# Four convolution layers on eight images: the stores of an image moved into its last convolution, and the matmuls of a strip pair put in another order

## What is computed

```
x = x + irfftn(complex 3x3 convolution of rfftn(norm(x)))   # layer 0
x = x + gate(norm(x))                                       # layer 1: rows and halves of the channels are let through or not
x = x + conv3x3(norm(x), W)                                 # layer 2
x = x + conv3x3(norm(x), weight)                            # layer 3
```

## Time and profile before, and how to read them

| | kernel before |
|---|---|
| median of three runs | 4691.74 us |
| the profiled execution's own time | 4709.38 us |
| its span, from the first to the last instruction | 4707.6 us |
| TensorE busy | 4279.1 us (91% of the span) |
| VectorE busy | 3334.5 us (71%) |
| ScalarE busy | 2540.4 us (54%) |
| mean granted TensorE clock | 0.971 of full speed |
| data read and written in HBM | 323.60 MB and 134.22 MB |

### The profile page before, as it was taken

The page is one execution under the profiler, slowest core; times in us unless marked ns, Lnnn a source line. Parts: engine busy times, 40 slices in busy tenths (PEclk is TensorE's granted clock), DMA queues, the critical chain, the costliest instruction groups (busy, mean ns, idle before and its releaser), DMA issues.

```text
span 4707.6 us, 229463 instructions
## 1 busy us (share of the span) xinstructions
PE 4279.1 (91%) x85024; PEld 2675.9 (57%) x85024; DVE 3334.5 (71%) x13348; ACT 2540.4 (54%) x8637; POOL 1.0 (0%) x6
## 2 busy tenths in 40 slices
PE   4999988999999998999989999899998999988898
PEld 1455765556655566555655566555665557655476
DVE  2887757876578765887658875688756887578863
ACT  4675526655266543666436654366633666345562
POOL 0000000000000000000000000000000000000000
PEclk8999999999999999999999999999999999999999
DMA  7442015620155202651035510356003650034204
GB/s 190 130 136 76 4 40 171 189 89 4 49 185 182 74 3 62 187 186 54 3 85 183 183 38 3 94 181 187 27 3 108 186 181 14 3 109 139 88 4 146
DMA packets 290246, 468.06 MB, mean 99 GB/s; under 512 B 25536, under 2 KB 92288, under 8 KB 289408
## 3 DMA queue, kind: packets, MB, share of 16 engines
q1 hardware_dynamic: 289536, 457.92, 32.4%
HBM read 323.60 MB, written 134.22 MB: 97 GB/s over the span
## 4 chain that ended last, share of the span: by engine, by line
PE 60%; DVE 12%; DMA 8%; issue 8%; SPq 5%; ACT 3%; DVEq 1%; ACTq 1%
PE ps L1361 34%; PE ps L1255 9%; DMA raw<-x 8%; PE ps L1270 5%; PE ps L1263 3%; PE ps L1279 3%; PE ps L1125 2%; DVE shared L858 2%; SPq L426 2%; SPq L433 2%; DVE xin L853 1%; DVE shared L854 1%; SPq L407 1%; ACT x L584 1%; DVE xin L852 1%
## 5 line engine op out<-in xcount | busy, mean ns | idle before, releaser
L1361 PE MATMUL ps<-x,conv_s 32*32 32x512 f32 x49104 | 1741.9, 606 | 62.4 <-DVE x L1087 30.0
L1361 PEld LDWEIGHTS ps<-x,conv_s 32*32 32x32 f32 x49104 | 1242.5, 104 | 509.5 <-issue 273.7
L1255 PE MATMUL ps<-shared 32*32 32x512 f32 x16384 | 657.4, 604 | 0.0
L1270 PEld LDWEIGHTS ps<-hil,shared 128*128 128x128 f32 x4096 | 504.6, 194 | 194.0 <-issue 193.2
L662 ACT ACTIVATE x<-ps,vec 128x256 f32<-128x256 f32 x512 | 214.6, 470 | 741.4 <-PE ps L1361 741.4
L584 ACT ACTIVATE x<-ps,vec 128x128 f32 (+1 forms) x1024 | 377.6, 385 | 432.2 <-PE ps L1270 431.2
L858 DVE SCALAR_TENSOR_TENSOR shared<-xin,trig 128x128 f32<-128x128 f32 x2048 | 533.8, 301 | 106.7 <-DVE shared L854 98.8
L1279 PE MATMUL ps<-eye,vsb 128*128 128x128 f32 x2048 | 370.7, 305 | 237.1 <-DVE vsb L879 134.1
L1270 PE MATMUL ps<-hil,shared 128*128 128x128 f32 x4096 | 572.5, 284 | 0.0
L1086 DVE SCALAR_TENSOR_TENSOR x<-ps,x 128x256 f32<-128x256 f32 x512 | 214.8, 420 | 427.2 <-ACT x L662 426.2
L1255 PEld LDWEIGHTS ps<-shared 32*32 32x32 f32 x16384 | 310.3, 104 | 278.8 <-issue 213.2
(11 more groups left out here) (204 smaller groups left out, 4711.7 us busy)
## 6 DMA issues: line engine op xcount, KB each, us to landing
out<-x SPq DMA_DIRECT2D x512, 256.0 KB
shared<-x SPq DMA_DIRECT2D x448, 256.0 KB
raw<-x SPq DMA_DIRECT2D x256, 256.0 KB
raw<-x SPq DMA_DIRECT2D x512, 128.0 KB
shared<-t_strip SPq DMA_DIRECT2D x512, 96.0 KB, 4.0
x<-x SPq DMA_DIRECT2D x64, 256.0 KB, 8.8
x<-t_proj SPq DMA_DIRECT2D x1, 2048.0 KB, 11.8
trig<-t_trig SPq DMA_DIRECT2D x1, 512.0 KB, 12.1
```

The costliest lines, as they stand in the source:

```text
L1255: mm = pe.matmul(ps[TM * cg:TM * cg + TM, bank, :], wst[TM * rg:TM * rg + TM, k, v, a, :], of[TM * rg:TM * rg + TM, :], start=(a == AXS), ...
L1270: mm = pe.matmul(quarter(ps[:, BY + 2 * odd + e, :], int(q < 2), q % 2), xt[:, e, q, :], hil[:, q, 0:P], start=False, stop=True, skip_grou ...
L1361: mm = pe.matmul(halves(ps[TM * cg:TM * cg + TM, banks[k], :]), conv_s[TM * rg:TM * rg + TM, kw, second, :], x1b[TM * rg:TM * rg + TM, of, ...
```

## The change

It changes four things. SyncE: of an image's 64 strips, 56 are stored in its own third convolution and the last 8 in the next first layer; the loads of the next image's pairs 0, 1 and 2 stand before the first store, after 36 stores and after 48 stores. TensorE: `add_u` takes one strip, and the order is, for each strip, row term, Hilbert product, transposes; the wait for the eviction stands before each strip's first products in `mix`. ScalarE: `turned_out` of the first strip stands before both `evict`. VectorE: in `make_planes`, `minus` is made before `plus`, the full wait at the weights becomes a wait for all but the last step, and the next image's planes are made at pairs 17 and 23 of the third convolution.

```
--- before.py
+++ after.py
@@ -27,7 +27,8 @@
 GROUPS = STRIPS // GROUP
 STORE_SEMS = 4
 STORES = 16 * STRIPS // STORE_SEMS
-DEFERRED = STRIPS - 2 * UNROLL
+DEFERRED = 2 * UNROLL
+STORED_BY = (36, 48, STRIPS - DEFERRED)
 SIDE = HALF + 2
 WIDE = 2 * SIDE
 PAIRS = STRIPS // 2
@@ -39,7 +40,7 @@
 GATES_AHEAD = 3 * GROUP
 GATE_STEPS = 3 * GROUP + 2
 RAW = 2
-U_AT, C_AT, PLANES_AT = (5, 8), (12, 14, 16), (20, 22)
+U_AT, C_AT, PLANES_AT = (5, 8), (12, 14, 16), (17, 23)
 DOT_CREDIT = 2
 
 
@@ -416,14 +417,13 @@
             for k in range(STORE_SEMS):
                 sp.sem_inc(c_stored[k], STORES)
 
-            def store(i, s):
-
-                k = s % STORE_SEMS
+            def store(i, s, k, turn):
+
                 sp.wait_ge(evicted, ev(i, 1 + STRIPS + s + 1))
                 sp.sem_inc(s_sp, 1)
-                sp.wait_ge(c_stored[k], (i + 1) * STORES + s // STORE_SEMS * 16)
+                sp.wait_ge(c_stored[k], (i + 1) * STORES + turn * 16)
                 sp.sem_inc(s_sp, 1)
-                sp.dma_start(out[i].rearrange("c (s r) w -> s r c w", r=ROWS)[s], x1[:, s, 0:N]).then_inc(c_stored[k], 16)
+                sp.dma_start(out[i].rearrange("c (s r) w -> s r c w", r=ROWS)[s], x1[:, bass.ds(s, 1), 0:N]).then_inc(c_stored[k], 16)
 
             def load_next(image, s, t, k):
 
@@ -438,7 +438,7 @@
                     sp.wait_ge(a_projected, j * LANDING + (k - LANDING + 1 + A_CREDIT))
                     land(j * LANDING + k, k)
 
-            for pair in range(2):
+            for pair in range(AHEAD):
                 load_pair(0, pair, 2 * pair)
 
             def image(i, more, stores_left):
@@ -454,27 +454,27 @@
                 if more:
                     sp.wait_ge(p_cols, 3 * i + 1)
                     sp.sem_inc(s_sp, 1)
-                for pair in range(2, AHEAD):
-                    load_pair(i, pair, 2 * pair)
-                for pair in range(DEFERRED // 2):
+                for pair in range(PAIRS):
                     feed(pair, 2 * pair % TABLES)
-                    if stores_left:
+                    if stores_left and pair < DEFERRED // 2:
                         for e in range(2):
-                            store(i - 1, STRIPS - DEFERRED + pair * 2 + e)
-                for pair in range(PAIRS - UNROLL, PAIRS):
-                    feed(pair, 2 * pair % TABLES)
+                            s = STRIPS - DEFERRED + pair * 2 + e
+                            store(i - 1, s, s % STORE_SEMS, s // STORE_SEMS)
+
+                def stores(first, last):
+
+                    with sp.Fori(first // STORE_SEMS, last // STORE_SEMS) as j:
+                        for k in range(STORE_SEMS):
+                            store(i, j * STORE_SEMS + k, k, j)
+
                 if more:
-                    for pair in range(2):
+                    stored = 0
+                    for pair, until in enumerate(STORED_BY):
                         load_pair(i + 1, pair, 2 * pair)
-
-                for n in range(PAIRS):
-                    if more and n >= PAIRS - (STRIPS - DEFERRED):
-                        sp.wait_ge(evicted, ev(i, 1 + STRIPS + 2 * n + 2))
-                        sp.sem_inc(s_sp, 1)
-                        store(i, n - (PAIRS - (STRIPS - DEFERRED)))
-                    elif not more:
-                        for e in range(2):
-                            store(i, 2 * n + e)
+                        stores(stored, until)
+                        stored = until
+                else:
+                    stores(0, STRIPS)
 
             image(0, True, False)
             with sp.Fori(1, B - 1) as i:
@@ -608,9 +608,10 @@
                 def step(t, odd, uses):
 
                     copy_v(t)
+                    turned_out(t * 2, 0)
                     for e in range(2):
                         evict(t * 2 - 2 + e, e, BY + 2 * (1 - odd) + e, 2 * (1 - odd) + e, uses)
-                        turned_out(t * 2 + e, e)
+                    turned_out(t * 2 + 1, 1)
                     squares(t * 2 - 2, 2 * (1 - odd), uses)
 
                 copy_v(0)
@@ -849,17 +850,20 @@
                     dve.wait_ge(x_loaded[e], (i * PAIRS + pair + 1) * (16 + 16 * e))
                     dve.wait_ge(mixed, i * PAIRS + pair - 1 + MIXED_CREDIT)
                     plus, minus = xin[:, k, 0:HALF], xin[:, k, HALF:N]
-                    b.did(V.scalar_tensor_tensor(plus, raw[:, e, 0:HALF], v1(MEAN2), raw[:, e, HALF:N], ALU.subtract, ALU.add))
-                    V.tensor_tensor(minus, raw[:, e, 0:HALF], raw[:, e, HALF:N], ALU.subtract).then_inc(x_taken, 1)
-                    b.then(V.scalar_tensor_tensor(fg(wst[:, k]), fg(mix_s[:, 1]), row_trig[:, 0, bass.ds(s, 1)], fg(mix_s[:, 0]), ALU.mult, ALU.add))
-                    dve.wait_ge(x_taken, i * STRIPS + s + 1 + RAW)
+                    b.did(V.tensor_tensor(minus, raw[:, e, 0:HALF], raw[:, e, HALF:N], ALU.subtract))
+                    V.scalar_tensor_tensor(plus, raw[:, e, 0:HALF], v1(MEAN2), raw[:, e, HALF:N], ALU.subtract, ALU.add).then_inc(x_taken, 1)
+                    b.did(V.scalar_tensor_tensor(fg(wst[:, k]), fg(mix_s[:, 1]), row_trig[:, 0, bass.ds(s, 1)], fg(mix_s[:, 0]), ALU.mult, ALU.add))
+                    b.settle(but=1)
                     for a in range(2):
                         for q in range(2):
                             b.did(V.scalar_tensor_tensor(quarter(planes[:, a, k, :], q, 0), split_in(minus)[:, q, :], 1.0, split_in(trig[:, a, 0:HALF])[:, q, :],
                                                          ALU.mult, ALU.mult, accum_out=gsum[:, 2 * a + q, bass.ds(s, 1)]))
+                        if a == 0:
+                            dve.wait_ge(x_taken, i * STRIPS + s + 1 + RAW)
                         ins = V.tensor_tensor(planes[:, a, k, HALF:N], plus, trig[:, a, 0:HALF], ALU.mult)
                         if a == 0:
                             b.did(ins)
+                            b.settle(but=3)
                             b.did(V.scalar_tensor_tensor(fg(wst[:, k]), fg(mix_s[:, 2]), row_trig[:, 1, bass.ds(s, 1)], fg(wst[:, k]), ALU.mult, ALU.add))
                     ins.then_inc(planes_ready, 1)
                     assert b.n == DVE_B, b.n
@@ -1239,13 +1243,14 @@
 
                     pe.wait_ge(planes_ready, t0 + t * 2 + 2)
                     due()
-                    pe.wait_ge(y_evicted, t0 + t * 2 - 2) if type(t) is not int or t > 1 else None
-                    due()
                     for e in range(2):
                         pe.wait_ge(v_copied[e], i * PAIRS + t) if type(t) is not int or t > 0 else None
                         due()
                     for a in (AXS, AXB, AXC):
                         for e in range(2):
+                            if a == AXS and (type(t) is not int or t > 1):
+                                pe.wait_ge(y_evicted, t0 + t * 2 - 3 + e)
+                                due()
                             k = 2 * odd + e
                             for v in range(2):
                                 for rg in range(TILES):
@@ -1256,12 +1261,11 @@
                                                    start=(a == AXS), stop=(v == 1 and a == AXC), skip_group_check=True)
                     mm.then_inc(mixed, 1)
 
-                def add_u(t, odd, table, uses):
-
-                    for e in range(2):
-                        pe.wait_ge(tab_loaded[table + e], (i * (STRIPS // TABLES) + uses + 1) * 16)
-                        pe.matmul(ps[:, BY + 2 * odd + e, :], strip[HP * e:HP * e + HP, table + e, 0:P], u[HP * e:HP * e + HP, :],
-                                  start=False, stop=False, skip_group_check=True)
+                def add_u(e, odd, table, uses):
+
+                    pe.wait_ge(tab_loaded[table + e], (i * (STRIPS // TABLES) + uses + 1) * 16)
+                    pe.matmul(ps[:, BY + 2 * odd + e, :], strip[HP * e:HP * e + HP, table + e, 0:P], u[HP * e:HP * e + HP, :],
+                              start=False, stop=False, skip_group_check=True)
 
                 def hilbert(s, e, odd):
 
@@ -1289,8 +1293,8 @@
                 def step(t, odd, uses, table, table_uses, first=False):
 
                     mix(t, odd)
-                    add_u(t - 1, 1 - odd, table, table_uses)
                     for e in range(2):
+                        add_u(e, 1 - odd, table, table_uses)
                         hilbert(t * 2 - 2 + e, e, 1 - odd)
                         turn(t, e)
                     project_next(2 * (1 - odd), table, uses, first)
@@ -1310,8 +1314,8 @@
                         step(j * 4 + 1 + k, (k + 1) % 2, j * 2 + k // 2, 2 * k, j)
                 for t in range(PAIRS - 3, PAIRS):
                     step(t, t % 2, (t - 1) // 2, 2 * (t - 1) % TABLES, STRIPS // TABLES - 1)
-                add_u(PAIRS - 1, 1, TABLES - 2, STRIPS // TABLES - 1)
                 for e in range(2):
+                    add_u(e, 1, TABLES - 2, STRIPS // TABLES - 1)
                     hilbert(STRIPS - 2 + e, e, 1)
```

## The result

The kernel after takes 4747.7 us (median of 4 runs, 4741.4 to 4751.9), the kernel before 4693.7 beside it (4 runs, 4676.9 to 4716.7). The ratio is 1.0104, with a 95% interval of 1.0076 to 1.0132: slower by some 50 us, twice the 23 us that a measurement can tell.

A forecast was written before the change was run, and what follows sets the result against it. TensorE, busy for 91% of the span, was taken as the bound. First layer -12.6, third-convolution stores +41 and planes +26 gave +54 us: 4763.8 against the profiled execution, 4746 against the median; range 4620 to 4805.

The forecast's parts named there:

- The row terms apart: First layer, TensorE: each strip's row term runs alone at 1.06 us, making the step 9.6 us.
- the second row term is cheap: Rival, first layer: the second term costs less than its 1.06 us; 4623 at half, 4499 at nothing; chance 0.20.
- ScalarE's order: First layer: copying the first transposes before the evictions ends the waits on L577; later evictions cost nothing in images 0 to 6.
- I leave 0.15 of it: First layer of image 7: of mix's 0.90 and 0.98 us wait for the second eviction, 0.15 stays; step 8.74.
- The first two intervals: Start of the first layer, images 1 to 6: the first two mix-to-mix intervals stay at 23.4 us together.
- The stores in the third convolution: Third convolution, images 0 to 6: TensorE stalls among the stores, 5.9 us an image, 41 in seven.
- likeliest reading: Third convolution: TensorE's six unexplained stalls in image 7, 6.7 us, are code fetches coming late among the stores.
- fetches stay hidden: Rival, third convolution: code fetches cost nothing, so without the 41 us the kernel takes 4705; chance 0.17.
- stores starve the third convolution: Rival, third convolution: stalls three times image 7's and late pair 1 planes, 82 us more, 4828; chance 0.10.
- The planes apart: Third convolution: planes at pairs 17 and 23 cost two waits and clock falls, 3.7 us an image, 26 in seven.
- Planes fit: Rival, third convolution: with the blocks apart both waits vanish, -40 in place of +26 us, 4680; chance 0.08.
- VectorE's wait at nothing: First layer: removing VectorE's full wait, 0.39 us a pair, gains nothing unless the step came below 8.4 us.

The follow-up runs named there:

- experiment 1: The changed kernel with both strips' row terms ahead of the first Hilbert product again, all else as changed: 4565.4 us, 0.972 of the kernel before.
- Experiment 2: The changed kernel with the DMA queue's order of before, 56 strips stored in the next first layer: 4788.4 us, 1.0188 of the kernel before.
- experiment 8: The changed kernel with the row terms together again and two stores in flight in place of four: 4700.7 us, 0.998 of the kernel before.
- experiment 3: The changed kernel with the next image's planes at pairs 20 and 22 again: 4727.9 us, 1.0056 of the kernel before.
- Experiment 10: The changed kernel with row terms together, planes at pairs 20 and 22, and VectorE's planes in the order and full wait of before: 4598.3 us, 0.9786.

## Why the forecast held, and which of its terms did not

4746 us were forecast and 4747.7 measured. The closeness is partly luck: the main mechanism was sized right, several errors of 10 to 25 us cancel, and the profiled executions are 42.5 us apart where the medians are 54.

**The row terms apart: right.** 1.06 a strip was forecast, 1.06 and 1.05 came; the group doubled as told. The step is 9.66 for 9.6; the 0.06 lies in mix, 3.41 for 3.33, whose first products take 1.31 us for 1.14. Between them the divided wait now stands; that it is the cause was not tried. The rival "the second row term is cheap" is refuted by experiment 1. Its price, though, was too high: with the term free I had put the kernel at 4499, and it came to 4565. The even step fell by 0.91 us in place of 1.06, 35 us in 233 steps, and the uneven steps of images 1 to 6, where the transposes wait for VectorE's copy, make up nearly 30.

**ScalarE's order: right for images 0 to 6, wrong for image 7, 17 us.** "I leave 0.15 of it" was the step that failed: the pitch of image 7 is 9.47, not 8.74. TensorE in image 7, and ScalarE at the same time:

```profile
4304.93 1.16 PE L1274 MATMUL ps<-hil,shared 128*128 128x128 f32 x8
4305.92 0.64 PE L1283 MATMUL ps<-eye,vsb 128*128 128x128 f32 x4
4306.49 1.70 PE L1260 MATMUL ps<-xin,shared 32*32 32x512 f32 x24
4307.59 0.69 PE L1260 MATMUL ps<-shared 32*32 32x512 f32 x8
```

```profile
4306.30 0.38 ACT L584 ACTIVATE x<-ps,vec 128x128 f32 x1 [0.61 <-PE ps L1274]
...
4307.00 0.38 ACT L586 ACTIVATE x<-ps 128x256 f32 x1
```

The eviction of the second strip cannot begin before its Hilbert product ends, whatever stands first on ScalarE, and takes until 4307.38; the second strip's products begin at 4307.53, inside the line with x24. Only the transposes and the first strip's products lie between, and mix takes 4.23 us in place of 3.41. No row calls this a wait, because the first strip's products run on meanwhile. I had taken the wait for a matter of ScalarE's order alone, and dividing it for its end. Where the projection stands between, as in images 0 to 6, it is covered, as told.

**The first two intervals: wrong, 4 to 6 us an image.** I left them at 23.4. In image 2 they are 1309.45 - 1290.11 = 19.3, and 17.5 to 19.4 in images 1 to 6. Experiment 2, with the old queue, has up to 28.1: it is the old queue that held the first pairs up, with pair 2 loaded late and the stores among the loads. Steps 0.08 too long over 29 intervals take back 2.3 of it in each image; together -31.0 for -15.6.

**Behind the last mix: left out.** I counted from mix to mix. The last step and the closing one have a split row term too: from the last mix to the closing row term it is 9.58 in image 2 where it was 9.11, and the closing one adds another 1.05. 7 x (0.47 + 1.05) = 10.6 accounts for the +10.3 of the table.

**The stores in the third convolution: mechanism right, term mis-sized.** The waits on issue appeared in images that had none (of images 0 to 6 before, only image 4 has 1.1 us), and experiment 2 takes them away. But they are 10.3 us over images 0 to 6 (0.5 in image 5, 3.7 in the worst), not 41. With everything that the stores do there it is 16: the seven third convolutions take 863.0 us after and 846.6 in experiment 2. The part beyond the waits on issue has no explanation here.

That these waits are for code, the "likeliest reading", can be read from the DMA packets of the trace. In the window of image 7 the instruction queue q8 brings 23 packets of 16 KB (packets, MB, share of 16 engines):

```profile
q8 instruction: 23, 0.38, 1.4%
```

Taken one by one, six of them start 5.8 to 6.6 us behind the one before, the others 3.4 to 5.0. Each of TensorE's six stalls ends 1.3 to 1.7 us behind the landing of one of these six late packets; over the whole run this holds for 18 of 19 stalls on issue. So TensorE waits for code there. A late packet need not cost anything: in image 5 before, distances of 6 to 10 us pass without a stall. That the stores have to do with it has experiments 2 and 8 for it: with the stores moved back no stalls in images 0 to 6, with fewer stores in flight 1.4 us for 6.2 in image 7. How they do it stays open. Image 5 moves 137 GB/s and image 7 147, so the rate alone does not part them; why image 7 meets so much more of it, 7.3 us, was not tried. The Trainium skill, page "Runtime: NRT & Kernel Launch", section "Instruction fetch mechanics", says that the crossing from one 16 KiB block of code to the next is mostly hidden; the trace agrees without stores, nearly so in images 0 to 6 with 1.5 us each, and not in image 7. On the waits alone the rival "fetches stay hidden" was nearer than the forecast, and "stores starve the third convolution" far off.

**The planes apart: right.** In image 5 two waits of some 3.4 us stand in place of 3.4 and 0.6, as the second block now meets a TensorE that has not been held back. Image 5 shows it most clearly; over images 0 to 6 these waits grow from 30.0 to 37.8 us, and without stores, in experiment 2, to 45.3. TensorE's granted clock is at 1.2 GHz for 24 us of these seven convolutions before, for 41 us after and in experiment 2. In image 5 both dips of the clock are there, in the windows of 4 us at the end of each wait, against the earlier trace rows (the figure before the DMA share is the clock: 0.66 and 0.65, means over stretches at 1.2 and at 2.4 GHz):

```profile
3563.00:3567.00 4.00, 3.21 (x66) 1.69 (x68) 1.97 (x6) 0.00 (x0) 0.00 (x0) 0.66 0.52 157
3587.00:3591.00 4.00, 3.33 (x66) 1.80 (x68) 1.85 (x6) 0.00 (x0) 0.00 (x0) 0.65 0.57 169
```

Without stores, the third convolutions of images 0 to 6 are 21 us longer with the planes apart (846.6 in experiment 2, 825.2 before, VectorE's shorter planes included); 26 were forecast. Beside the stores it is less: experiment 3 gives 13 back there. The two terms aren't independent; read in that order the stores cost 24.5 us and the planes 13.3 (read by experiment 2, 16.4 and 21.4). "Planes fit" is refuted either way.

**VectorE's wait at nothing: right beside a step of 9.66 us by the forecast's own condition only.** I had put the point from which it counts at a step of 8.4. Experiment 10 shows 46 us at steps of 8.9. In the profiled executions 21 us lie in the first two intervals of images 1 to 6. That VectorE works behind late loads there, which a mean over the steps hides, is my reading of it.

Summed in the forecast's terms: first layer -7.4 for -12.6, stores 16 for 41, planes 21 for 26, behind the last mix 10, ends 1.7: 42 for 54.

## What to carry to other kernels

Before a pair of half-height products is taken apart, look whether the group's busy time is half of count times duration: if so, they run side by side, and breaking up the pair costs nearly a full product each time, here 0.91 of 1.06 us and 180 us in all. A change of several parts is worth splitting: moving the stores out of the loading stage was worth 100 us with the terms together, and the reordering that came with it buried that. When a pitch is computed from one loop mark to the next, add the prologue and the closing half-step, and for each variant of the loop (here without projection) follow anew what covers each wait.

## What was not expected of the hardware

With four stores in flight TensorE stood idle on issue for 6.2 us of a convolution with written-out code, with two for 1.4, and the stalls end 1.3 to 1.7 us behind the landing of late 16 KB packets of code; yet two in flight needed 146.6 us for 63 stores, 2.3 us each, and the queue ended 53 us behind the last eviction. In image 5 a second block of VectorE work of the same size cost TensorE 0.6 us when it came two pairs behind the first, and 3.4 us when it came six pairs behind.
